# Crossbar transposes issued from ScalarE's queue, four transpose buffers, and a shorter mask and digit path in a recommendation kernel

## What is computed

```
item_emb = concat(table_i1[item0], table_i2[item1], table_i3[item2])        # 96
ub       = concat(table_i1[his0],  table_i2[his1],  table_i3[his2])         # 200 x 96
att_in   = concat(q, ub, q - ub, q * ub)                                    # q = item_emb
score    = (att_in @ w_att1.T + b_att1) @ w_att2.T + b_att2
score    = where(his0 == 0, 0, score)
browse   = sum over positions of score * ub
x = dice(concat(item_emb, browse, user_emb) @ w1.T + b1)
x = dice(x @ w2.T + b2);  out = sigmoid(x @ w3.T + b3)
```

## Time and profile before

| What | Value |
|---|---|
| median of 3 runs | 1636.73 us (1633.69 to 1641.48) |
| the profiled execution: its own time / its span | 1642.58 us / 1640.7 us |
| VectorE busy | 1470.9 us, 90% of the span |
| TensorE busy | 1344.9 us, 82%; mean granted clock 0.923 |
| GpSimd busy | 1316.8 us, 80% |
| ScalarE busy | 744.5 us, 45% |
| first matmul of the main loop / last step's sums collected | 52.85 us / 1593.7 us |

### The profile page before, as it was taken

One profiled execution on the slowest core, in us unless ns is written; L12 is line 12 of the kernel. 1 busy time (PEld: TensorE's weight loads), 2 busy tenths in 40 slices (PEclk: granted clock), 3 DMA queues, 4 the chain that ended last, 5 costly groups with the idle time before them and its releaser, 6 DMA issues. The chain is left out here.

```text
span 1640.7 us, 68361 instructions
## 1 busy us (share of the span) xinstructions
PE 1344.9 (82%) x26911; PEld 1239.5 (76%) x26911; DVE 1470.9 (90%) x1579; ACT 744.5 (45%) x1601; POOL 1316.8 (80%) x1924
## 2 busy tenths in 40 slices
PE   5587978879797987969889797979879797887965
PEld 4476968778687877869788786868778787876851
DVE  7699999989999898989989899998989999898955
ACT  4453544535354453534445353444535344452326
POOL 3598988879788888978879798888979898896840
PEclk9899999989999998989899998999989899997976
DMA  2667566675746667566666756666675756757630
GB/s 29 141 105 146 100 141 116 112 156 108 152 97 129 125 108 160 108 139 99 128 131 111 158 105 146 100 125 131 113 155 105 149 97 134 127 112 145 114 78 0
DMA packets 507882, 194.21 MB, mean 118 GB/s; under 512 B 483526, under 2 KB 491318, under 8 KB 507646
## 3 DMA queue, kind: packets, MB, share of 16 engines
q1 hardware_dynamic: 500550, 188.83, 59.4%
q0 software_dynamic: 2144, 1.36, 0.8%
q10 hardware_dynamic: 4952, 0.28, 0.2%
HBM read 8.45 MB, written 1.44 MB: 6 GB/s over the span
## 5 line engine op out<-in xcount | busy, mean ns | idle before, releaser
L785 ACT ACTIVATE wsum_ring<-wsum_ps 128x300 f32<-128x300 f32 x512 | 359.7, 703 | 696.8 <-PE wsum_ps L580 694.8
L566 PEld LDWEIGHTS sel<-scoretab,hiT 128*128 128x128 bf16 x12288 | 518.0, 102 | 203.8 <-issue 161.9
L566 PE MATMUL sel<-scoretab,hiT 128*128 128x75 bf16 x12288 | 552.7, 204 | 145.3 <-DMA hiT<-onehot_hi 74.7
L580 PE MATMUL wsum_ps<-scaled_lo,onehot_hi 100*128 100x75 bf16 x12288 | 568.0, 204 | 97.7 <-DVE scaled_lo L1010 97.0
L580 PEld LDWEIGHTS wsum_ps<-scaled_lo,onehot_hi 100*128 100x128 bf16 x12288 | 522.7, 102 | 118.0 <-DVE scaled_lo L1010 111.6
L1010 DVE TENSOR_TENSOR scaled_lo<-onehot_lo,parts 100x3744 bf16<-100x3744 bf16 x256 | 540.2, 2110 | 64.2 <-POOL parts L475 54.7
L998 DVE TENSOR_REDUCE score_j<-sel 100x24 f32<-100x600 f32 x512 | 396.0, 774 | 60.5 <-PE sel L566 59.9
L464 POOL TENSOR_TENSOR score<-score,score_j 100x16 f32<-100x16 f32 x256 | 324.5, 1268 | 20.2 <-POOL score L461 0.2
L461 POOL TENSOR_TENSOR score<-score_j 100x16 f32<-100x16 f32 x256 | 200.1, 782 | 138.1 <-DVE score_j L998 136.8
L966 DVE TENSOR_TENSOR onehot_hi<-digits,iota_hi 100x1920 bf16<-100x1920 bf16 x256 | 295.1, 1153 | 3.0 <-PE wsum_ps L580 2.5
L793 ACT ACTIVATE scores_b<-acc 128x512 bf16<-128x512 f32 (+1 forms) x318 | 261.4, 822 | 2.4 <-PE acc L599 1.1
(11 more groups left out here) (156 smaller groups left out, 747.4 us busy)
## 6 DMA issues: line engine op xcount, KB each, us to landing
scoretab<-scores_b SPq DMA_DIRECT2D x192, 187.5 KB
weightsum<-wsum_ring SPq DMA_DIRECT2D x128, 125.0 KB
weightsum<-wsum_ring SPq DMA_DIRECT2D x64, 150.0 KB
raw<-in_r_rec_his_dram SPq DMA_DIRECT2D x32, 150.0 KB
hiT<-onehot_hi SPq DMA_TRANSPOSE x256
x_rows<-x_tile SPq DMA_DIRECT2D x14, 100.0 KB
scores_b<-x_rows SPq DMA_DIRECT2D x1, 1400.0 KB
item_rows<-in_L_rec_table_i_dram,ids_now POOLq DMA_INDIRECT x51
```

The costliest lines, as they stand in the source:

```text
L566: mm = pe.matmul(o, rows, scoretab[0:HJ, s // 16, :, b, i, :], start=(i == 0), stop=(i == 2))
L580: mm = pe.matmul(wsum_ps[:, s % 2, b * W:(b + 1) * W].rearrange("p (j v) -> p j v", j=NF), hi_columns(ring_slot(n), g), scaled_lo[:, n % 2 ...
L785: act.activation(wsum_ring[:, (s // 8) % 2, :, 4 * (s % 8):4 * (s % 8) + 4] .rearrange("p u b -> p b u"), wsum_ps[:, s % 2, 0:4 * W].rearr ...
```

## The change

1. **Queue.** `turn_hi`, with its waits, moves from Sync's program to ScalarE's, to the odd slots behind `copy_sums` and ahead of the copy of the table piece. All other direct DMAs of the loop stay on Sync.
2. **Four buffers.** `hiT` has four instead of two; the transpose of step n + 2 then waits for the matmuls of step n - 2 instead of step n. It is still issued two steps ahead.
3. **Pieces.** The next table goes over in five pieces (16, 16, 32, 32 and 32 users) instead of four of 32; TensorE makes it in slots 7 to 27 instead of 4 to 28; Sync's order is new, without transposes between.
4. **Mask.** `keep` is gone (two VectorE operations per half tile, two GpSimd operations per step that multiply by it, one of which wrote `parts`). The high digit is made one greater and multiplied by min(id, 1) of the first feature, so a masked position matches no high digit.
5. **Digits.** Five VectorE operations per half tile become three, and one goes to ScalarE (`scale_raw`, slots 8 and 23).
6. **Chain.** `split` has six operations and two waits between instead of seven and three.
7. **Finish** in slots 9 to 15 (7 parts) instead of 8 to 16 (9 parts). The set-up is reordered: the attention weights come before the digits and before the zeroing of `onehot_hi`'s rim.

```diff
-        hiT = sb("hiT", [128, 2, PER * POSP + 128 - POSP], BF16)
+        hiT = sb("hiT", [128, 4, PER * POSP + 128 - POSP], BF16)
...
         FIN = ["finish", "layer1"]
-        PARTS = 9
-        FIN_SLOT = 8
+        PARTS = 7
...
+        ROWS = (0, 16, 32, 64, 96, 128)
...
-                split_at[4 + len(split_at)] = (r, piece)
+            for piece in ("all", 1, 2):
+                split_at[7 + len(split_at)] = (r, piece)
         SPLIT_DONE = 3 * NR
...
                 await_ge(split_copied, SPLIT_DONE * (t + 1))
+                b0, b1 = ROWS[c], ROWS[c + 1]
                 if isinstance(t, int) and t == 0:
-                    sp.wait_ge(scoretab_zero, c // 2 + 1)
+                    sp.wait_ge(scoretab_zero, b0 // HALF + 1)
                 else:
...
-                    if n + AHEAD < STEPS:
-                        turn_hi(t, n + AHEAD)
-                    elif not last:
-                        turn_hi(t + 1, n + AHEAD - STEPS)
-                    if n == 0:
-                        place_scores(t, 3)
-                    if n in (1, 9) and not last:
-                        load_rows(2 * t + 2 + n // 9)
+                    if n == 14 and not last:
+                        place_scores(t + 1, 0)
+                    if n < 2:
+                        place_scores(t, 3 + n)
                     if n == 2 and not (isinstance(t, int) and t == 0):
                         collect_sums(t - 1, 3)
-                    if n == 8:
-                        collect_sums(t, 0)
-                    if n == 10:
-                        collect_sums(t, 1)
+                    if n in (8, 10):
+                        collect_sums(t, n // 2 - 4)
+                    if n == 14:
+                        collect_sums(t, 2)
+                    if n in (2, 9) and not last:
+                        load_rows(2 * t + 2 + n // 9)
                     if n == 11 and not last and not (isinstance(t, int) and t == 0):
                         keep_x1(t - 1)
                     if n == 11 and last:
                         sp.wait_ge(x1_out, 16 * (TILES - 2))
-                        sp.wait_ge(scoretab_in[3], TILES * NF * 16)
...
                         sp.dma_start(x1[:, :, 0:(TILES - 2) * TILE], x1_rows[:, :, 0:(TILES - 2) * TILE]).then_inc(x1_in, 16)
-                    if n == 14 and not last:
-                        place_scores(t + 1, 0)
-                    if n == 14:
-                        collect_sums(t, 2)
-                    if n == 15 and not last:
-                        place_scores(t + 1, 1)
-                        place_scores(t + 1, 2)
+                    if n >= 14 and not last:
+                        place_scores(t + 1, n - 13)
...
+                third = score_j[:, p2, :, 2]
+                pool.tensor_tensor(score_2[:, :], score_j[:, p2, :, 0], score_j[:, p2, :, 1], ALU.add
+                                   ).then_inc(parts_step, 1)
                 if not (isinstance(k, int) and k < 2):
...
-                kp = keep[:, hb, g0:g0 + PER]
...
-                    return ap.unsqueeze(2).to_broadcast([POS, PER, 2])
-
-                pool.tensor_tensor(score_2[:, :], score_j[:, p2, :, 0], score_j[:, p2, :, 1], ALU.add
+                pool.wait_ge(parts_step, 3 * k + 1)
...
+                pool.wait_ge(parts_step, 3 * k + 2)
+                pool.tensor_tensor(score_r[:, :], score[:, :], parts[:, p2, :, 0, 0], ALU.subtract)
+                pool.tensor_tensor(parts[:, p2, :, 1, :], twice(score[:, :]), parts[:, p2, :, 0, :], ALU.subtract
                                    ).then_inc(parts_step, 1)
...
-                    pe.wait_ge(hiT_in[s // 2 % 2], 16 * (t * (STEPS // 2) + s // 4 + 1))
-                if s % 8 == 0:
...
+
+                    pe.wait_ge(scoretab_in[ROWS.index(4 * s)], (t + 1) * (NF * 16))
...
+                act.wait_ge(signal, value)
+                if not isinstance(value, int):
+                    act.sem_inc(act_passed, 1)
+
+            def turn_hi(t, n):
+
+                k = t * STEPS + n
+                await_ge(hi_ready, k + 1)
+                await_ge(lo_rows_ready, k + 1)
+                if not (isinstance(k, int) and k < 4):
+                    await_ge(sel_full, 2 * k - 6)
+                act.dma_start(hiT[:, n % 4, 0:PER * POSP].rearrange("p (g l) -> p g l", g=PER),
+                             onehot_hi[:, ring_slot(n), :, :].rearrange("p g h -> p (g h)"), transpose=True
+                             ).then_inc(hiT_in[n % 4], 16)
+
+            def scale_raw(h):
+
+                act.wait_ge(raw_in, 16 * (h + 1))
+                act.activation(raw_f[:, :], raw[:, :], ACT.Identity, bias=offset[:, :], scale=1.0 / LO
+                               ).then_inc(raw_f_ready, 1)
             def lo_rows(t, n):
...
                 rows = onehot_hi[0:POS, ring_slot(n), :, 1:1 + 2 * NF].rearrange("p g (j i) -> p g j i", i=2)
-                act.activation(rows[:, :, :, 0], low, ACT.Copy)
-                act.activation(rows[:, :, :, 1], low, ACT.Square).then_inc(lo_rows_ready, 1)
+                act.activation(rows[:, :, :, 0], low, ACT.Identity, bias=centre[:, :])
+                act.activation(rows[:, :, :, 1], low, ACT.Square, bias=centre[:, :]).then_inc(lo_rows_ready, 1)
...
                     lo_rows(t + 1, ahead - STEPS)
+                if s % 2 and s // 2 + AHEAD < STEPS:
+                    turn_hi(t, s // 2 + AHEAD)
+                elif s % 2 and not last:
+                    turn_hi(t + 1, s // 2 + AHEAD - STEPS)
+                if s in (8, 23) and not last:
+                    scale_raw(2 * t + 2 + s // 23)
                 if s == SLOTS - 2 and not last and not (isinstance(t, int) and t == 0):
...
                 ins.then_inc(scaled_ready, 1)
-            def make_keep(t, hb):
-
-                if isinstance(t, int) and t == 0 and hb == 0:
...
-                    dve.wait_ge(parts_ready, (t - 1) * STEPS + 8 * hb + 8)
-                d = [digits[:, hb, k, :, NF - 1, 0] for k in range(2)]
-                dve.tensor_tensor(keep[:, hb, :], d[0], d[1], ALU.add).then_inc(keep_step, 1)
-                dve.wait_ge(keep_step, 2 * t + hb + 1)
-                dve.tensor_scalar(keep[:, hb, :], keep[:, hb, :], -float(MID), None, ALU.is_gt
...
             def make_digits(h, op, taken):
                 if op == 0:
-                    dve.wait_ge(raw_in, (h + 1) * 16)
-                    dve.tensor_scalar(raw_f[:, :], raw[:, :], -float(MID), None, ALU.add).then_inc(raw_f_ready, 1)
+                    dve.wait_ge(raw_f_ready, h + 1)
...
-                    dve.tensor_scalar(digit_f, raw_f[:, :], 1.0 / LO, ROUND, ALU.mult, ALU.add
-                                      ).then_inc(digit_step, 1)
-                elif op == 2:
                     if not (isinstance(taken, int) and taken == 0):
                         dve.wait_ge(task_full, taken)
-                    dve.wait_ge(digit_step, 2 * h + 1)
-                    dve.tensor_scalar(digits_b[:, 1, :], digit_f, -ROUND, None, ALU.add
-                                      ).then_inc(digits_b_ready, 1)
-                elif op == 3:
-                    dve.wait_ge(digits_b_ready, 2 * h + 1)
-                    dve.tensor_scalar(digit_f, digit_f, -ROUND, float(LO), ALU.add, ALU.mult
-                                      ).then_inc(digit_step, 1)
+                    dve.wait_ge(digit_hi_ready, h + 1)
+                    first = raw[:, :].rearrange("p (l f) -> p l f", f=NF)[:, :, 0:1].to_broadcast([2 * HALF, POS, NF])
...
-                                      ).then_inc(digits_b_ready, 1)
+                    dve.scalar_tensor_tensor(digits_b[:, 0, :], digit_hi[:, :], -float(LO), raw[:, :], ALU.mult, ALU.add
+                                             ).then_inc(digits_b_ready, 1)
             def step(t, n, last=False):
...
-                if 11 <= n <= 15 and not last:
-                    make_digits(2 * t + 3, n - 11, task_before(t, 21) + 1)
+                if 5 <= n <= 7 and not last:
+                    make_digits(2 * t + 2, n - 5, task_before(t, 3) + 1)
...
                 elif not (isinstance(t, int) and t == 0):
                     scale(t - 1, STEPS - 1)
+            dve.memset(centre[:, :], float(LO - MID)).then_inc(bias_ready, 1)
```

More of the change, by code:

```diff
@@ L181, in build @@
         scoretab_clear = sem("scoretab_clear")
-        scoretab_in = [sem(f"scoretab_in{c}") for c in range(4)]
+        scoretab_in = [sem(f"scoretab_in{c}") for c in range(5)]
         weightsum_in = sem("weightsum_in")
@@ L259, in build @@
         LAST_FIN = tasks_start(TILES - 1) + len(IN_LAST)
-        CHUNK = TILE // 4
+        ROWS = (0, 16, 32, 64, 96, 128)
+        CHUNKS = len(ROWS) - 1
         split_at = {}
         for r, (l0, l1) in enumerate(ROUNDS):
-            for piece in ("first", "rest", 1, 2) if l1 - l0 == 4 else ("all", 1, 2):
-                split_at[4 + len(split_at)] = (r, piece)
+            for piece in ("all", 1, 2):
+                split_at[7 + len(split_at)] = (r, piece)
```

(37 more changed lines are left out.)

97 lines of the change are left out of this document (45 added, 52 removed).

## The result

The changed kernel took 1785.57 us in the median of four runs (1765.87 to 1809.04) against 1639.11 before. I had forecast 1548 us. The profiled execution took 1777.6 us, span 1775.8.

A forecast was written before the change was run, and what follows sets the result against it. The prediction took VectorE as the bound: 1640.7 - 17.5 - 14.4 - 36 - 35 - 6 + 20 = 1551.8 us of span, adjusted to a forecast of 1548 us; its own range 1525 to 1575, the wider range 1508 to 1620.

The forecast's parts named there:

- Mask and digits: On VectorE, two mask operations go (-17.5 us) and the digit operations get shorter (-14.4 us).
- Chain: In GpSimd's chain, fewer operations and waits per step cut VectorE's 54.7 us of waits for `parts`: -36 us.
- Pieces and their order: Queue, pieces and four buffers together cut VectorE's 49.6 us of waits for `sel`, mostly at tile changes: -35 us.
- Set-up: Before the loop, attention weights ahead of the zeroing and digits let TensorE start earlier: -6 us, bounds -2 and -8.
- The transposes no longer stand behind pieces.: At the change of tile, transposes leave Sync's queue of table pieces; counted within the -35 us.
- What ScalarE pays: Transpose issues in ScalarE's queue delay its copies for TensorE: 1.25 us a tile, +20 us, bounds 0 and +60.
- Slower: ScalarE becomes the bound outright if an issue there costs above 3.2 us; 1720 us at 3.5 us, chance 0.07.
- Rival one: ScalarE and TensorE take the bound in slots with table pieces, 3.5 us a tile: 1604 us, chance 0.17.
- rival two: Transfers stay late because TensorE waits for the DMA engines, so VectorE's `sel` waits stay: 1583 us, chance 0.12.
- no change: Both rivals' costs together, with digit operations costlier: 1649 us at the most, somewhat less about 1637; chance 0.03.

The follow-up runs named there:

- e1: The changed kernel with the queue alone undone, the transposes issued by Sync again: 1585.67 us, 0.9675 of the kernel before.
- e3: The changed kernel with Sync issuing one table piece a step, each behind TensorE's first read of that step: 1774.66 us, 1.0844 of the kernel before.
- e4: The changed kernel, transposes from ScalarE, with pieces of one user instead of 16 or 32 from the second tile on: 1645.57 us, 1.0016 of the kernel before.
- e12: e1 with ScalarE in odd slots waiting for the transpose's semaphores, then running two chained copies: 1591.54 us, 0.9685 of the kernel before.
- e7: e1 with ScalarE in odd slots waiting for the transpose's semaphores, then running four chained copies: 1662.30 us, 1.0149 of the kernel before.
- e10: The changed kernel with each piece described as runs of 4 users (600 bytes), same bytes and issues: 1791.69 us, 1.0889 of the kernel before.

## Why the prediction was wrong

The queue costs 186 us where I had charged 20 and counted on a gain. Without the 20, my forecast for e1 would have been 1528 us, and it took 1585.67, so the rest was off too, by 58. Step by step, with e1 (all but the queue) for the steps that have nothing to do with it:

- *Mask and digits, -31.9.* Right: VectorE's busy time fell by 32.8 us in e1. The new operations on two tensors are as long as the row that I took, 455 ns:

```profile
L1041 DVE SCALAR_TENSOR_TENSOR digits_b<-raw,digit_hi 128x300 bf16<-128x300 int32 x32 | 14.6, 458 | 0.1
L1045 DVE SCALAR_TENSOR_TENSOR digits_b<-digit_hi,raw 128x300 bf16<-128x300 bf16 x32 | 14.6, 457 | 0.0
```

- *Chain, -36.* Right: the wait for `parts` went from 54.7 to 20.5 us in e1, -34.
- *Pieces and their order, -35.* Right as far as it is the pieces: VectorE's wait for `sel` went from 59.9 to 26.2 us in e1, with the transposes still on Sync. Without the first wait of each (10.3 and 8.0, which belong to the set-up) it is 49.6 to 18.2, -31.
- *Set-up, -6.* About half: the first maximum starts 3 us earlier in e1, at 51.57 instead of 54.57.
- *Not foreseen:* once VectorE is quicker it waits for TensorE's sums before `onehot_high`, 37.2 us in e1 and 2.5 in the kernel before:

```profile
DVE onehot_hi L966 <- PE wsum_ps L580: 2.5, 6, 1.1
```

I had read that TensorE works 30.69 of 32 us in the "finish" stretch and charged it only within the 20 us. Those five make 32.8 + 34 + 31 + 3 - 35 = 66 us, and e1's span is 64.5 us shorter.
- *"The transposes no longer stand behind pieces."* This is the step that failed, and in sign. They stand beside them on a second queue, for which I had no price, and that is worse: 99 us more for the same traffic. I had quoted the rule "Issuing engines are not separate DMA queues" of the Trainium skill's "DMA: Bandwidth & Descriptors" as one by which the wait would merely stay, 35 us. The runs agree with it in that the second queue didn't take the transfers out of each other's way, and go further: the second queue made the transposes later than one queue did, 14.4 us against 6.0 in the two places shown. The rows of the DMA queues fit. After, in two queues, the packets took 48.9 + 15.8 = 64.7% of 1775.8 us, 1149 us; in e1 the same number of packets, all but 4952 of the set-up in one queue, took 62.4 + 0.2 = 62.6% of 1576.2, 987 us (packets, MB, share of 16 engines; the changed kernel, then e1):

```profile
q10 hardware_dynamic: 471896, 117.76, 48.9%
q1 hardware_dynamic: 36006, 71.36, 15.8%
```
```profile
q1 hardware_dynamic: 502950, 188.83, 62.4%
...
q10 hardware_dynamic: 4952, 0.28, 0.2%
```

- *What ScalarE pays, +20.* The mechanism was right, the size was not: 82 to 88 us. I had added the issues to ScalarE's busy time and found 73 of 90 us, room enough. But the price lies in one slot, not in the sum of a tile: issue 1.55, copy, then TensorE's next piece, which has one bank. The 1.24 us of idle time in the earlier trace rows was the number to set against 1.57; I read it and set it against "one issue in two slots". The difference, 0.33 us in each of 254 odd slots, would be 84 us. That agrees with the hold, but it is one slot's idle time, and such times in that tile lie between 0 and 2.9 us, so it is an estimate. The issues themselves took 34 us a tile (543 / 16) instead of 28.
- *The chances.* "Slower" had 0.07, by an issue above 3.2 us. The issue's median on ScalarE was 1.63 us and its mean 2.1; that mechanism didn't happen. What happened were rivals one and two together, on top of the 58 us by which e1 missed. Rival one came near its price, 20 + 56 = 76 us against 82 to 88; rival two cost nearly three times its own, 99 against 35. I had let the two reach only "no change".

## What to carry to other kernels

A DMA issue on a compute engine costs its time at the place where it stands in that engine's order: compare it with the idle time of that slot, not with the engine's busy share. Moving one kind of transfer to another queue doesn't take it out of the others' way. That one queue had kept the urgent transposes in turn with the pieces, and that the second let twelve pieces' transfers go ahead of them, is my reading of the timelines; pacing the pieces (e3) didn't win the time back, so it isn't shown. Here the parts of the change without the queue, e1, are the better kernel: 0.9675 of the time before.

## What the runs showed of the hardware

- A transpose ((471896 - 4952) / 256 = 1824 packets, 114 on each of the 16 DMA engines if they are spread evenly) landed 14.4 us after its issue began beside twelve transfers of the other queue, in the changed kernel. In the kernel before, one queue with them, its like took 6.0 us.
- The issue itself is longer beside such traffic: on ScalarE's queue it took between 1.53 and 11.54 us, median 1.63, where Sync's was 1.46 to 4.82, median 1.57. Ten issues took over 4 us, eight of them at changes of tile; with the small pieces of e4 only two did, both in the last tile.

```profile
L841 ACTq DMA_TRANSPOSE hiT<-onehot_hi x256: 1525/1626/11542, 41.6 to 1706.1; - x128
```

- A hold of ScalarE of 0.74 us in every other slot (e12) cost nothing that can be measured, and one of 1.59 us (e7) cost 82 us: 254 holds, 0.32 us each in the mean, so some 1.3 us of each was still hidden.
- Describing the pieces as runs of 600 bytes instead of 2400 and 4800 (e10) left the number of packets at 510281.
- After 9.04 us without work TensorE ran at a granted clock of 0.50, its lower level, until 807 us, and 24 matmuls took 1.70 us instead of 1.01.
